# A decoder layer: the weights' preparation in the prologue re-cut in halves and spread over three engines

## The reference

```
x = x + attention(layernorm(x))          # weights rounded to -1, 0, 1 times one scale, activations to 8 bits
x = x + gated_convolution(layernorm(x))  # the second block: products, a long causal convolution, products
x = x + ffn(layernorm(x))                # the third block: weights rounded to fp8
```

```
s  = 1.0 / clip(mean(abs(w)), 1e-5)      # one s for q, k and v together, another one for the output weights
wq = clip(round(w * s), -1, 1) / s
```

## Time and profile before

| | us |
|---|---|
| median of 3 executions | 1489.31 (1488.61 to 1491.14) |
| the profiled execution | 1488.82 |
| its span, first instruction to last | 1487.0 |
| PE busy | 1390.5 |
| DVE busy | 1234.5 |
| ACT busy | 871.8 |
| POOL busy | 1177.6 |
| part 1 ends at about | 480 |

### The profile page before, as it was taken

One profiled execution on the slowest core, in us unless ns is written; L12 is line 12 of the kernel. 1 busy time (PEld: TensorE's weight loads), 2 busy tenths in 40 slices (PEclk: granted clock), 3 DMA queues, 4 the chain that ended last, 5 costly groups with the idle time before them and its releaser, 6 DMA issues.

```text
span 1487.0 us, 23871 instructions
## 1 busy us (share of the span) xinstructions
PE 1390.5 (94%) x8327; PEld 775.5 (52%) x8405; DVE 1234.5 (83%) x1964; ACT 871.8 (59%) x1437; POOL 1177.6 (79%) x902
## 2 busy tenths in 40 slices
PE   3698999999986898899999999999999999999998
PEld 2577787878764443334444444444444444444443
DVE  6789999999984799789898899899889888888611
ACT  5589999999886223444545455455456446544341
POOL 3279999999985687888888878878887888788532
PEclk9799999999998899999999999999999999999999
DMA  5545565655431533222422331332323232240001
GB/s 191 132 111 152 139 167 139 167 139 152 127 83 58 175 100 81 68 50 71 100 50 52 91 78 43 79 78 64 78 64 71 62 81 50 68 102 15 18 19 29
DMA packets 171587, 133.57 MB, mean 90 GB/s; under 512 B 120500, under 2 KB 124748, under 8 KB 171468
## 3 DMA queue, kind: packets, MB, share of 16 engines
q1 hardware_dynamic: 171276, 131.91, 35.4%
q10 hardware_dynamic: 192, 0.14, 0.0%
HBM read 50.67 MB, written 19.92 MB: 47 GB/s over the span
## 4 chain that ended last, share of the span: by engine, by line
PE 64%; DVE 12%; POOL 8%; issue 7%; ACT 7%; DMA 1%; SPq 0%; POOLq 0%; DVEq 0%; ACTq 0%
PE gu L839 20%; PE gu L853 10%; PE shared_bank L784 9%; POOL pL L1782 3%; PE y L806 3%; PE y L800 3%; PE y L803 3%; PE y L808 3%; PE y L809 3%; DVE blockmax L980 2%; DVE o_sb L1020 2%; DVE z L1210 1%; DVE qkt L960 1%; PE s_kq L632 1%; ACT pH L1427 1%
## 5 line engine op out<-in xcount | busy, mean ns | idle before, releaser
L1654 ACT ACTIVATE shared<-shared_bank 128x512 f32<-128x512 f32 x162 | 96.1, 593 | 320.5 <-PE shared_bank L784 320.5
L1207 DVE TENSOR_TENSOR y<-shared,y 128x512 f32<-128x512 f32 x324 | 223.9, 691 | 41.2 <-ACT shared L1654 22.1
L1782 POOL TENSOR_TENSOR pL<-pT,pH 128x768 f16<-128x768 f32 x128 | 217.0, 1698 | 12.9 <-ACT pH L1427 7.4
L839 PE MATMUL gu<-fT,wg 128*128 128x512 f16 x768 | 181.4, 379 | 1.5 <-DMA fT<-fnl 1.5
L1214 DVE TENSOR_REDUCE oT<-z 128x64 f32<-128x512 f32 x256 | 175.6, 686 | 8.7
L839 PE MATMUL gu<-fT,wu 128*128 128x512 f16 x768 | 182.2, 380 | 0.0
L1210 DVE TENSOR_TENSOR z<-y,cT 128x512 f32<-128x512 f32 x236 | 162.3, 688 | 10.7 <-PE y L798 4.4
L1916 POOL TENSOR_TENSOR fuL<-fu,fuH 128x512 f16<-128x512 f32 x96 | 112.0, 1167 | 71.8 <-ACT fuH L1669 71.6
L853 PE MATMUL gu<-wd,fuL 128*128 128x512 f16 x384 | 145.6, 379 | 0.0
L853 PE MATMUL gu<-wd,fuH 128*128 128x512 f16 x384 | 145.6, 379 | 0.0
L1852 POOL TENSOR_TENSOR kv<-vT,cT 128x1024 f32<-128x1024 f32 x70 | 137.8, 1970 | 5.9 <-ACT vT L1609 5.9
(11 more groups left out here) (222 smaller groups left out, 3540.2 us busy)
## 6 DMA issues: line engine op xcount, KB each, us to landing
pack<-qkhl SPq DMA_DIRECT2D x256, 128.0 KB, 2.6
x_sb<-in_x SPq DMA_DIRECT2D x16, 512.0 KB, 4.0
c_sb<-in_ctx SPq DMA_DIRECT2D x32, 256.0 KB, 4.0
hankel<-in_L_xattn_k SPq DMA_DIRECT2D x32, 256.0 KB, 4.1
out_y<-yo SPq DMA_DIRECT2D x32, 256.0 KB, 2.9
x_grp<-x_scratch SPq DMA_DIRECT2D x30, 256.0 KB, 3.5
x_scratch<-x_sb SPq DMA_DIRECT2D x14, 512.0 KB, 3.0
wraw<-in_L_attn_w_qkv SPq DMA_DIRECT2D x3, 1024.0 KB, 9.6
```

What stands on the lines that cost most here:

```text
L839: made = T.matmul(bank[:], (wg, wu)[which][:, cb, ib * P:(ib + 1) * P], fT[:, cb, part, :], start=cb == 0 and part == 0, stop=cb == CB - 1 ...
L1207: chain.step(V.tensor_tensor(bank[:], shared[2 * part + half][:], bank[:], op))
L1782: G.tensor_tensor(pL[n % 2][:], pT[n % NP][:], pH[n % NP][:], ALU.subtract).then_inc(low_done, 1)
```

## The change

Six things change, all of them before step 20.

- q's and k's weights are made ternary, turned and copied in halves (blocks 0, 1 and blocks 2, 3), and the four products of the first batch stand between the halves, in the order q low half, k low half, k high half, q high half. k's turned blocks and q's last two are copied by DVE, q's first two by ACT.
- v's weights are made ternary by three GpSimd instructions (`ternary_v`) and no longer by DVE.
- The sum over the output weights is taken by ScalarE (`magnitude(3, 0, 4)`) and no longer by DVE, and their scale is worked out before the steps.
- The input statistics of batches 1, 2 and 3 (`stats_in`) stand together behind the first batch's low halves, where batch 1's stood between the weights' copies and the first scaling.
- For the first batch's eight pairs the scores for the maximum go to `s_qk` and `s_kq` in turn, and wait only for the maximum of two pairs ago.
- The output weights are turned in steps 2 and 4 instead of 1 and 2, the first load of a piece is in step 5 instead of 3, and piece 0 starts two steps later: masked in 8, taken in 18, stored in 19.

The core of the diff:

```diff
-        V_WEIGHTS_AT, PROJ_WEIGHTS_AT, LOAD_PIECES_AT = (-1, 0), (1, 2), 3
-        OUT_SCALE_AT, OUT_SIGN_AT = -1, 0
+        V_WEIGHTS_AT, PROJ_WEIGHTS_AT, LOAD_PIECES_AT = (-1, 0), (2, 4), 5
+        OUT_SIGN_AT = 0
...
-            return n if k == (0 if n else 4) and 0 <= n < PIECES else None
+            return n if k == (0 if n else 6) and 0 <= n < PIECES else None
...
-            return i == 0 or (i >= 2 and ob % 2 == 0)
+            return (i == 0 and ob < 2) or (i >= 2 and ob % 2 == 0)
...
-            return s % 2, 2 * (s // 2)
+            return ((0, 0), (1, 0), (1, 2), (0, 2))[s]
+
+        def score_tile(n):
+            return s_kq if n < PAIRS and n % 2 == 1 else s_qk
...
-                w.wait_ge(max_done, n)
+                w.wait_ge(max_done, max(n - 1, 0) if n < PAIRS else n)
...                                              # PE
-            turn_weights(1)
-            turn_weights(0)
+            turn_weights(1, (0, 1))
             spread_c(0)
-            for g2 in range(4):
-                multiply_qk(0, g2)
+            turn_weights(0, (0, 1))
+            multiply_qk(0, 0)
+            multiply_qk(0, 1)
+            turn_weights(1, (2, 3))
+            multiply_qk(0, 2)
+            turn_weights(0, (2, 3))
+            multiply_qk(0, 3)
+            weight_total(4, 1, 1)
...                                              # DVE
-            ternary(1)
+            ternary_k(0)
+            ternary_k(1)
+            copy_weights(1, (0, 1))
...
-            copy_weights(1)
-            stats_in(1)
-            for g2 in range(4):
-                scale_qk(0, g2)
+            scale_qk(0, 0)
+            copy_weights(1, (2, 3))
+            scale_qk(0, 1)
+            copy_weights(0, (2, 3))
+            scale_qk(0, 2)
+            scale_qk(0, 3)
             for g2 in FIRST_LOW_ON_DVE:
                 low_first(g2)
+            stats_in(1)
+            stats_in(2)
             max_in(1)
             scale_in(1)
-            magnitude(3, WB, 4)
-            ternary(2)
+            weight_scale(1, 1, 2, 1)
...
+            stats_in(3)
...                                              # ACT
+            sign_weights(0, 1, slice(2, 4))
+            for g2 in range(4):
+                high_qk(0, g2)
+            magnitude(3, 0, 4)
             moments(1)
-            high_qk(0, 0)
-            high_qk(0, 1)
-            high_qk(0, 2)
-            high_qk(0, 3)
             normalise(1)
...                                              # POOL
+            def ternary_v():
+                w.wait_ge(wscale_done, 1)
+                chain.step(G.tensor_scalar(wraw[2][:], wraw[2][:], ws[:, 1:2], ROUND, ALU.mult, ALU.add))
+                chain.wait()
+                chain.step(G.tensor_scalar(wraw[2][:], wraw[2][:], ROUND - 1.0, ROUND + 1.0, ALU.max, ALU.min))
+                chain.wait()
+                w.wait_ge(wtr_pe, w_turned(0, WB - 1))
+                G.tensor_scalar(tern[0][:], wraw[2][:], ROUND, None, ALU.subtract).then_inc(tern_pool, 1)
...
-            power_in(1)
             for g2 in range(4):
                 if g2 not in FIRST_LOW_ON_DVE:
                     low_qk(0, g2)
+            power_in(1)
+            ternary_v()
```

More of the change, by code:

```diff
@@ L364, in decoder_kernel, with wT_copied @@
         W_ORDER = (1, 0, 2, 3)
+        W_TURNS = [(1, 0), (1, 1), (0, 0), (0, 1), (1, 2), (1, 3), (0, 2), (0, 3)] + [(i, ob) for i in (2, 3) for ob in range(WB)]
         def wT_by_act(i, ob):
-            return i == 0 or (i >= 2 and ob % 2 == 0)
[L370 to L374, removed]
+            return (i == 0 and ob < 2) or (i >= 2 and ob % 2 == 0)
+        def wT_copied(i, ob):
+            by_act = wT_by_act(i, ob)
+            return sum(wT_by_act(*at) == by_act for at in W_TURNS[:W_TURNS.index((i, ob)) + 1])
         def w_turned(i, ob):
-            return WB * W_ORDER.index(i) + ob + 1
+            return W_TURNS.index((i, ob)) + 1
         def low_made(n):
@@ L391, in turning, with wT_ready @@
                     yield i, range(2 * at.index(t), 2 * at.index(t) + 2)
-        def wT_ready(w, i):
-            w.wait_ge(wT_act, wT_copies(i, WB - 1, True))
-            w.wait_ge(wT_dve, wT_copies(i, WB - 1, False))
+        def wT_ready(w, i, blocks=range(WB)):
+            for ob in blocks:
+                w.wait_ge(wT_act if wT_by_act(i, ob) else wT_dve, wT_copied(i, ob))
         def qk_groups(s):
-            return s % 2, 2 * (s // 2)
+            return ((0, 0), (1, 0), (1, 2), (0, 2))[s]
+        def score_tile(n):
+            return s_kq if n < PAIRS and n % 2 == 1 else s_qk
         def wait_packed(w, b):
@@ L926, in weight_scale, with ternary_k @@
                 V.reciprocal(ws[:, at + 1:at + 2], ws[:, at:at + 1]).then_inc(wscale_done, 1)
-            def ternary(i):
+            def ternary_k(half):
+                part = slice(2 * half, 2 * half + 2)
                 w.wait_ge(wscale_done, 1)
                 w.wait_ge(wsum_act, 2)
-                chain.step(V.tensor_scalar(wraw[i][:], wraw[i][:], ws[:, 1:2], ROUND, ALU.mult, ALU.add))
+                chain.step(V.tensor_scalar(wraw[1][:, part, :], wraw[1][:, part, :], ws[:, 1:2], ROUND, ALU.mult, ALU.add))
                 chain.wait()
-                chain.step(V.tensor_scalar(wraw[i][:], wraw[i][:], ROUND - 1.0, ROUND + 1.0, ALU.max, ALU.min))
+                chain.step(V.tensor_scalar(wraw[1][:, part, :], wraw[1][:, part, :], ROUND - 1.0, ROUND + 1.0, ALU.max, ALU.min))
                 chain.wait()
-                if i == 2:
-                    w.wait_ge(wtr_pe, w_turned(0, WB - 1))
-                V.tensor_scalar(tern[i % 2][:], wraw[i][:], ROUND, None, ALU.subtract).then_inc(tern_dve, 1)
+                V.tensor_scalar(tern[1][:, part, :], wraw[1][:, part, :], ROUND, None, ALU.subtract).then_inc(tern_dve, 1)
             def copy_weights(i, blocks=range(WB)):
@@ L1122, in vector_program @@
                     copy_weights(i, blocks)
-                if t == OUT_SCALE_AT + 1:
-                    weight_scale(1, 1, 2, 1)
-                    w.wait_ge(wscale_done, 3)
-                    chain.step(V.tensor_tensor(ws[:, 5:6], ws[:, 0:1], ws[:, 2:3], ALU.mult))
                 for use, k in halves(t):
@@ L1142, in vector_program @@
                 for b, k in batches(t, NORM_AT, LOAD_AHEAD + 11, 2):
-                    if k == LOAD_AHEAD:
+                    if k == LOAD_AHEAD and b > 3:
                         stats_in(b)
```

60 lines of the change are left out of this document (30 added, 30 removed).

## The result

The changed kernel takes 1510.13 us (median of 4 runs, 1507.59 to 1511.85) beside 1488.96 us for the kernel before: 1.0139 times as long, 95% interval 1.012 to 1.0158, or 21 us more. The forecast was 1501.5 with a range of 1493 to 1508, so the time lies outside it. Slower was right, the stall at piece 2 was right, and the size was 9 us short. The profiled run took 1509.84 us, its span is 1508.0.

The account below looks back on a forecast made before the run. Part 1 was taken as a belt at POOL's pace, so early delays reach the end: +1.0 front, -2.5 freed POOL steps, +15.2 stall, -2.5 given back, +1.5 PE clock = +12.7 on 1488.8, 1501.5 us, range 1493 to 1508.

Parts of the forecast that it names:

- front to step 8, v hidden: Start to step 8: with v's ternary hidden on POOL, step 8's scores about +1.0 us late, between -2 and +5.
- v's ternary, to step 8: POOL before step 0: three one-input instructions taken as 6.5 us, done at 43.4, hidden behind batch 1's rounding; no cost.
- POOL's freed steps, step 8 to P: Steps 15 and 16: POOL no longer adds and takes piece 0, so P comes 2.5 us earlier (0 to -3.6).
- P: Moment when POOL ends batch 3's last low half and the fourth pack starts; 105.7 before the change.
- stall, in distance from P to the mask: Step 18: piece 2's load falls behind batch 3's pack on SP; mask at P + 16.0, was P + 0.8: +15.2 us.
- given back, and PE's clock: Behind the stall: 2.5 us won back by faster mask and shorter waits, +1.5 for PE at half clock.
- Batch 1 sets step 0: Front: batch 1's later statistics put its normalisation 5.5 us later, at 36.95; first scores about 50.9, +2.0.
- No stall of note, and the prologue gives what it looks like: Rival, the faster side: no stall at piece 2 and gains in the prologue give 1480 to 1485; chance 0.09.
- First batch's products: Prologue: halves bring the first scaling to 24.7 (27.5 before), but the fourth to 31.55 (30.17 before).
- rival of a cheap passing: SP's queue at step 18: passing the pack costs little, mask at P + 10.2, 5.8 us less, 1495.5; chance 0.09.
- From then on the belt is the same ... so it stays: After the stall: the same instructions at the same pace, so the +12.7 us shift stays to the end.
- v at a higher price on top of the stall: Rival: v's ternary on POOL at the two-input price, 11.7 us, adds 3.7 to the stall: 1505; chance 0.12.

Follow-up runs that it names:

- number 2: Changed kernel with v's three ternary instructions on DVE instead of GpSimd, behind batch 1's scaling; pieces stay late: 1504.37 us, 1.0106.
- number 3: Changed kernel with the weight pieces back in their old steps and v's ternary on DVE: 1493.61 us, 1.0029.
- number 1: Changed kernel with the pieces of the gate's and up weights, and the output weights' turning, back in their old steps: 1501.07 us, 1.008.
- number 4: Kernel before, with only the pieces of the gate's and up weights and the output weights' turning moved later as in the change: 1500.38 us, 1.0072.
- Number 8: Changed kernel without the maximum and minimum (clamp) of v's weights on GpSimd: 1503.4 us, 1.0097.
- Number 7: number 3 with batch 1's statistics, moments and power earlier, and the output weights' sum and scale reordered, the scale ahead of v's ternary: 1489.99 us, 1.0004.
- Number 5: Changed kernel with piece 0's store and piece 2's load issued ahead of batch 3's pack in SP's program: 1504.02 us, 1.0098.
- 11: Kernel before with the output weights' sum on ScalarE and all pieces but the first two steps later: 1516.51 us, 1.0187.
- 12: Kernel before with only the pieces after the first two steps later: 1518.07 us, 1.0197.
- 6: Kernel before with seven GpSimd instructions of 128x768, five times over, ahead of its second power, to price forms: one execution, 1552.4 us.
- 9: number 3 with one tile for the first batch's scores, as before, instead of two: 1493.69 us, 1.0035.
- 10: Kernel before with only the output weights' sum moved to ScalarE, and their scale on DVE right behind batch 1's scaling: 1489.02 us, 0.9998.

## Why the prediction was wrong in size

By the prediction's own terms, in shifts of POOL:

| term | forecast | measured |
|---|---|---|
| front to step 8, v hidden (number 2) | +1.0 | +2.1 |
| v's ternary, to step 8 (changed kernel less number 2) | 0 | +5.2 |
| POOL's freed steps, step 8 to P | -2.5 | -3.2 |
| stall, in distance from P to the mask | +15.2 | +16.2 |
| given back, and PE's clock | -1.0 | -1.9 |
| sum, at 200 us | +12.7 | +18.4 |
| junction of the parts, and last norm | 0 | +2.6 |

By parts of the change the same 18.4 us are 4.8 for batch 1's order with all the rest (number 3), 4.7 for v (number 1 less number 3), and 8.9 for the late pieces (the changed kernel less number 1); these include that piece 0's mask and clamp leave steps 6 and 7, where DVE is the bound, worth 2.2 at step 8 (number 4).

- **v's ternary: the step that failed.** "The instruction has one input, so I take 6.5: done at 43.4, hidden behind batch 1's rounding." It took 14.5 and ended at 52.95. The bounds were set by the number of inputs, from rows of an affine_select and a product of two tensors, and both ends lay below the truth; so rival and range, built on 11.7, did too. Only the first of the three forms costs what was assumed (1.97). The prediction's own sign of being wrong, "v's three instructions ending after 45", came true. Number 8 shows that the rest of the step was nearly sound: at 7.4 us it is hidden but for 0.6 us at step 0. The Trainium skill, GPSIMD Engine Reference, "Engine selection", says that GpSimd is about two times slower than VectorE for two inputs and runs "roughly line-rate" for one. The measurement decides: 128x2048 took VectorE 1.23 us for maximum and minimum and GpSimd 7.12.
- **Batch 1 sets step 0: right, and 2 us short.** The forecast had its normalisation at 36.95 (38.36 measured), its first scaling at 46.3 (46.89), the scores of step 0 at 50.9 and of step 8 at 75.0. With v out of the way (number 2) they come at 52.56 and 76.92. "No stall of note, and the prologue gives what it looks like" fell with number 3: batch 1 late costs 4.8 us, since ScalarE's queue, with the output weights in it, sets step 2, and step 8 follows at the old distance (16.7 us in both). Number 7 takes it back by order alone.
- **First batch's products: right in order, 1 to 1.5 us short.** Scalings forecast at 24.7 and 31.55, measured 25.65 and 33.09: an early first half and a late last one, of no value to the whole.
- **The stall: right in place, cause and size.** Forecast P + 16.0 for the mask, measured P + 17.0 (P is now 109.8), the load landing 4.9 us behind its issue and not 3.4. Number 5 parts the 16.2 us: 6.2 are for passing the pack (5.8 in the prediction's rival of a cheap passing, which falls), and the other 10.0 are for the two steps.
- **PE's clock: right in kind.** Half clock in the stall and 0.88 in the 5 us of the last window shown. How much of the -1.9 is the clock's was not separated.
- **"From then on the belt is the same ... so it stays": not quite.** The shift holds within 0.3 us through part 1. But at the last norm the changed kernel and numbers 1, 4, 5, 7, 11 and 12 lost another 1.7 to 3.2 us, with a clock of 0.50 to 0.75 in the 4 us behind the same pause; numbers 2, 3, 6, 8, 9 and 10 lost nothing, at full clock. The shifts ahead of it (0.4, 9.3, 9.5, 13.4, 19.0, 24.3 and 28.1 us against 0.8, 4.9, 5.0, 13.7, 15.4 and 63.6) show no order. What decides it is open; the profiles are one execution each, and the runs of one kernel differ by as much (1507.59 to 1511.85).

v's price is 5.2 of the 8.3 us by which the sum was short of the profiled executions (8.5 by the medians), the last norm and the junction 2.6. That the other terms were off by 0.5 us in all is partly luck: front and stall were about 1 us short each, and the freed steps and what was given back made up for most of it. Of the cases set out, v at a higher price on top of the stall was the true one; its price was too low there as well, and the range ended where it did for that reason. Two small slips in the prediction change nothing: 5.8 less than 1501.5 is 1495.7, and its low end, with 3 us off the front and 2.45 off the issue, is 1496.

## What to carry to other kernels

Before work is moved to another engine, price its very form there: which operations an instruction names, and not its inputs, set the cost on GpSimd here, by three times. In a belt with a full engine the place of a fixed piece of work within the period is worth more than the waits that it shows: two steps later cost 2.3 us in each batch. And a load that shares a queue with a long row of transfers should be followed in the queue's order, not by the program's steps.

## What was unexpected of the hardware

- GpSimd's forms: 0.91 us for multiply and add, 2.13 for a subtract or a maximum, 2.77 and 2.85 for two operations with a maximum, 1.80 for the sum of two tensors, all at 128x768.
- The neighbours slow each other. In the first pass of number 6 POOL's float32 subtract took 3.43 us and not 2.13, and DVE's 2048-wide maximum and minimum beside it took this (timeline of DVE), where the earlier trace rows have 1.23:

```profile
18.30 1.72 DVE L933 TENSOR_SCALAR wraw<-wraw 128x2048 f32<-128x2048 f32 x1
```

- In the changed kernel an operation of DVE on one element per partition took 2.87 us beside POOL's maximum and minimum (timeline of DVE). Its like took 0.53 before, 2.01 in number 8 beside POOL's subtract, and 0.16 in number 2, where POOL stood idle.

```profile
42.04 2.87 DVE L1132 TENSOR_TENSOR ws<-ws 128x1 f32<-128x1 f32 x1
```

- The same pause of PE of some 2 us was followed by a full clock in some runs and by half clock in others.
